# A two-stream decoder kernel: another merged order of the two streams' steps on every engine

## The reference

```python
# layer 0
x = LN(x + relu(softmax(causal(x Wq (x Wk)^T / 16))) (x Wv))             # "self"
x = LN(x + LN(softmax(mask(x Wq2 (ctx Wk2)^T / 16)) (ctx Wv2)) g + b)    # "cross"
x = LN(x + sign_mlp(x))            # 256 -> 1024 -> 1024 -> 256, weights +1/-1   "sign"
# layer 1
x = LN(x + causal_performer(x))    # 16 heads, 64 relu features, running sums   "perf"
x = LN(x + mlstm(x, ctx))          # 8 heads, exponential gates, group norm    "mlstm"
x = LN(x + ffn(x))                 # int8 rounding, 256 -> 1024, conv of 3, silu, -> 256  "quant"
```

## Time and profile before

| | |
|---|---|
| median of 3 runs | 868.52 us (868.14 to 871.88) |
| the profiled execution's own time | 874.67 us |
| its span, from the first to the last instruction | 873.4 us |
| PE busy | 757.4 us, 87% |
| DVE busy | 588.3 us, 67% |
| ACT / POOL busy | 368.2 us, 42% / 147.9 us, 17% |
| mean granted TensorE clock | 0.90 |

### The profile page before, as it was taken

How to read it: one execution, slowest core, us unless ns; L and a number is a source line. 1 busy time by engine, 2 the same in 40 slices (tenths; PEclk the granted TensorE clock), 3 DMA queues, 4 the chain that set the end, 5 groups by cost and what they waited for, 6 DMA issues and landing times.

```text
span 873.4 us, 14709 instructions
## 1 busy us (share of the span) xinstructions
PE 757.4 (87%) x5872; PEld 531.1 (61%) x5872; DVE 588.3 (67%) x1486; ACT 368.2 (42%) x659; POOL 147.9 (17%) x223
## 2 busy tenths in 40 slices
PE   9999999999999985779889999999999968668214
PEld 5776654575787774676564676676476846547102
DVE  2485864264546779987789856566365767778796
ACT  2564632123314625843338433343354125473183
POOL 5021100031000324102310020110014120113200
PEclk9999999999999995858899999999999968869565
DMA  9501000001000102003000030000000000000001
GB/s 353 189 1 73 1 1 0 1 2 44 8 2 2 26 1 73 25 25 96 1 1 0 2 96 2 2 1 2 1 2 1 2 1 2 0 2 2 0 12 36
DMA packets 12739, 23.75 MB, mean 27 GB/s; under 512 B 768, under 2 KB 7040, under 8 KB 12416
## 3 DMA queue, kind: packets, MB, share of 16 engines
q1 hardware_dynamic: 12672, 22.82, 7.6%
HBM read 20.72 MB, written 2.10 MB: 26 GB/s over the span
## 4 chain that ended last, share of the span: by engine, by line
PE 71%; DVE 20%; POOL 3%; issue 3%; ACT 2%; DVEq 0%; ACTq 0%
PE bank L719 13%; PE bank L543 7%; PE bank L535 5%; PE bank L567 5%; PE bank L588 5%; PE bank L810 3%; PE bank L729 3%; PE bank L792 3%; PE bank L707 2%; PE bank L760 2%; POOL small L2071 2%; DVE work L1630 2%; PE bank L1011 2%; DVE work L1624 2%; DVE stats L1121 1%
## 5 line engine op out<-in xcount | busy, mean ns | idle before, releaser
L2001 POOL TENSOR_TENSOR rstd<-rstd,minus_half 128x2 f32<-128x2 f32 x56 | 44.5, 795 | 458.7 <-DVE rstd L1127 458.5
L719 PE MATMUL bank<-work,f0w 128*128 128x512 f16 x512 | 112.8, 379 | 0.0
L719 PEld LDWEIGHTS bank<-work,f0w 128*128 128x128 f16 x512 | 50.1, 98 | 59.4 <-issue 0.8
L1337 DVE SCALAR_TENSOR_TENSOR work<-bank,work 128x512 f16<-128x512 f32 x64 | 42.2, 686 | 45.0 <-ACT work L1829 44.8
L1829 ACT ACTIVATE work<-bank 128x512 f16<-128x512 f32 x64 | 36.6, 596 | 74.8 <-PE bank L719 60.5
L588 PE MATMUL bank<-work 128*128 128x256 f32 x208 | 49.8, 382 | 0.0
L2071 POOL TENSOR_TENSOR small<-small,minus_half 128x8 f32<-128x8 f32 x16 | 27.7, 1729 | 105.2 <-DVE small L1560 105.2
L1011 PE MATMUL bank<-work 128*128 128x66 f32 (+1 forms) x256 | 36.8, 307 | 8.7 <-DVE work L1501 6.2
L1011 PEld LDWEIGHTS bank<-work 128*128 128x128 f32 x256 | 36.6, 227 | 10.3 <-issue 7.3
L588 PEld LDWEIGHTS bank<-work 128*128 128x128 f32 x208 | 37.4, 190 | 5.1 <-issue 0.8
L810 PE MATMUL bank<-work 64*128 64x128 f32 x512 | 38.7, 292 | 1.1 <-DVE work L1420 1.1
(11 more groups left out here) (296 smaller groups left out, 1771.4 us busy)
## 6 DMA issues: line engine op xcount, KB each, us to landing
work<-in_mask SPq DMA_DIRECT2D x4, 1024.0 KB, 8.8
xT<-in_xT SPq DMA_DIRECT2D x4, 512.0 KB, 5.2
ctxT<-in_ctxT SPq DMA_DIRECT2D x4, 512.0 KB, 5.9
perf_w<-in_k SPq DMA_DIRECT2D x3, 512.0 KB, 11.3
perf_w<-in_perf_w SPq DMA_DIRECT2D x1, 1536.0 KB, 6.0
ctx<-in_w SPq DMA_DIRECT2D x2, 512.0 KB, 14.0
work<-in_w SPq DMA_DIRECT2D x1, 1024.0 KB, 16.0
x<-in_x SPq DMA_DIRECT2D x2, 512.0 KB, 15.2
```

Of the source, the lines that this page charges most:

```text
L719: ins = nc.tensor.matmul(u.bank[:, :], f0w1[:, k, m * P:(m + 1) * P], s.h1[part][:, k, :], start=(k == 0 and part == 0), stop=(k == NF - 1 ...
L1337: low_part(what, m, dst, number + m, lambda o, x, hi: nc.vector.scalar_tensor_tensor(out=o, in0=x, scalar=0.0, in1=hi, op0=ALU.max, op1=AL ...
L2001: nc.gpsimd.tensor_tensor(s.rstd[:, two], s.rstd[:, two], minus_half[:, 0:2], ALU.pow).then_inc(s.rstd_made.sem, 1)
```

## The change

New texts for all five engines; nothing else. The diff's core, one line of each for two engines (the other lines are replaced in the same way):

```diff
 TURNS = {
     "tensor":
-        "a1 b1 a2 b3 a2 b1 a2 b1 a3 b1 a1 b2 a3 b4 a1 b1 a3 b3 a2 b2 a2 b3 a1 b5 a1 b5 a4 b1 a2 b2 a2 b3 a1 b7 a1 b1 "
+        "a5 b1 a6 b1 a2 b1 a5 b2 a2 b1 a13 b2 a1 b3 p1 a2 b2 a2 b2 a1 b1 a6 b1 a3 b2 a2 b1 a2 b1 a3 b1 a2 b3 a2 b1 a2 "
...
     "sync":
-        "w1 a1 w1 b1 w2 a1 w2 b1 w1 b2 a2 w1 a1 b1 a1 b1 a2 b2 a3 b3 a2 b2",
+        "w4 a1 w1 b1 a1 w1 a1 w1 b2 a1 b1 w1 b1 a6 b1 a1 b5 a2 b2",
```

More of the change, by code:

```diff
@@ L37 @@
     "tensor":
[8 rows of a table removed]
-    "vector":
[11 rows of a table removed]
-    "scalar":
[7 rows of a table removed]
[8 rows of a table added]
+    "vector":
[11 rows of a table added]
+    "scalar":
[8 rows of a table added]
     "gpsimd":
-        "a1 b1 a1 b1 a1 b5 a7 b1 a1 b3 a1 b1 a1 b1 a6 b3 a6 b3 a1 b1 a1 b3 a2 b1 a1 b1 a6 b1 a1 b1 a2 b3 a1 b4 a3 b2 "
-        "a1 b1 a1 b2 a5 b1 a2 b9 a1 b3 a1 b2",
+        "a7 b3 a5 b4 a4 b2 a1 b2 a1 b1 a5 b1 a2 b3 a2 b2 a2 b3 a1 b1 a1 b1 a3 b2 a1 b1 a1 b1 a3 b3 a1 b4 a3 b2 a1 b2 "
+        "a1 b1 a5 b1 a2 b10 a1 b2 a1 b2",
     "sync":
-        "w1 a1 w1 b1 w2 a1 w2 b1 w1 b2 a2 w1 a1 b1 a1 b1 a2 b2 a3 b3 a2 b2",
+        "w4 a1 w1 b1 a1 w1 a1 w1 b2 a1 b1 w1 b1 a6 b1 a1 b5 a2 b2",
 }
```

## The result

The changed kernel takes 866.4 us in the median of 20 runs (862.08 to 868.68), the old one 870.24 us (20 runs, 865.8 to 874.56). I had forecast 8 us, and 860.5.

A forecast was written before the change was run, and what follows sets the result against it. No single bound: sign and perf at PE's pace, mlstm and quant at DVE's. Gains of 5 us up to b1's start, 0 in the middle and 3 at the end made 8, from 868.5 to 860.5 us; range 846 to 876.

The forecast's parts named there:

- The step that failed: From b1's start at 516 to about 717 us: orders nearly the same, PE has work; 0, give or take 2 us.
- Term 1: The start: a0, nearly alone, reaches perf at about 133 us instead of 179.5, with 5 us added (bounds 2 and 12).
- The rival in which it loses 12 us: a0's lone start loses 12 us, not 5, using up the middle stretch's gain; within the no-difference rival, chance 0.22.
- Term 2: a0 through perf and mlstm: reaches `quant.turn0` at about 314 us instead of 345.3, 31 us earlier.
- Term 3: From a0's `quant.turn0` to b1's `self.score0`: most of the lead is lost, b1 starts 5 us earlier.
- Term 4: The end: a1's DVE work fills b1's gaps, 3 us earlier (bounds 0 and 7).
- the larger gain: The valley closes, DVE fed at 91% from a0's `quant.turn0` to b1's start; 845.5 us, chance 0.13.
- the slower one: a1's attention and b0's head steps hold each other up, DVE under 79% before b1's start; 878 us, chance 0.19.
- No difference that tells: Mixture before b1's start runs at 81%, or a0's lone start loses 12 us; about 867.5 us, chance 0.22.

The follow-up runs named there:

- e14: Changed kernel with the old order put back from a1's `quant.hidden0` to the end; ratio 1.0025 to the old kernel, 2.2 us slower.
- e1: Old kernel with the changed order only in round 0, up to b1's `self.q`; ratio 0.9972, 2.4 us faster.
- e4: Old kernel with the changed order in round 0 and from a1's `quant.hidden0` to the end, old between; ratio 0.9938, 5.4 us faster.
- e8: The old kernel run once more without edit, for a second trace; 870.24 us, span 869.0.
- e15: Changed kernel with the old order where b1's cross lies beside a1's perf, up to b1's `sign.a0`; ratio 0.9913 to the old kernel, 7.6 us faster.
- e13: Old kernel with the changed round 0, plus b1's `self.q` and `self.v` moved ahead on PE; ratio 0.9923, 6.7 us faster.
- S: Part of the change where b1's self lies beside a1's perf, up to b1's `cross.q1`; alone on the old kernel ratio 1.0046, 4.0 us slower.
- the two PE moves: On PE b1's `self.q` ahead of a1's `perf.xT0`, `self.v` ahead of `perf.v0` and `xT1`; alone on the old kernel ratio 1.0032, 2.8 us slower.
- H: Part of the change in round 0, up to b1's `self.q`; alone on the old kernel ratio 0.9972, 2.4 us faster.
- M: Part of the change from b1's `self.q` to a1's `quant.hidden0`; alone on the old kernel ratio 1.0089, 7.7 us slower.
- e3: Old kernel with the changed order only from a1's `quant.hidden0` to the end; ratio 0.9942, 5.0 us faster.
- T: Part of the change from a1's `quant.hidden0` to the end; alone on the old kernel ratio 0.9942, 5.0 us faster.

## Why the prediction missed

**The step that failed** is "From 516 to about 717 us both orders are the same but for steps moved by one or two places in a stretch in which PE has work: 0, give or take 2." Behind the new round 0 this part costs 4.6 us (e14 less e1), with the new tail as well 2.0 (changed kernel less e4), on the old order 7.7. The traces show it in the changed kernel: 4.9 us ahead at b1's `self.score0`, 0.2 at its `sign.a0`. The stretch between these two steps, all engines, first in e8, then in the changed kernel, then in e15:

```profile
512.90:594.00 81.10, 80.90 (x789) 56.91 (x788) 46.17 (x131) 29.50 (x62) 9.00 (x15) 1.00 0.01 1
...
508.00:594.00 86.00, 80.77 (x814) 57.79 (x820) 46.40 (x134) 29.49 (x61) 11.41 (x18) 1.00 0.01 2
...
508.50:592.00 83.50, 80.29 (x813) 57.69 (x821) 46.61 (x134) 29.52 (x61) 11.60 (x18) 1.00 0.01 2
```

PE is busy 80 to 81 us at full clock in all three, and idles 0.2, 5.2 and 3.2 us (some tenths of the last two can be matmuls whose record is missing). So in the old order PE did have work without a break, and "PE has work" was still no reason for zero: it had work because the steps were laid so that one stream's product covers the other's wait. e15 names one place and gives 4.2 us back. What e15 still idles, e13 does not (its lead is 5.5 us at `self.score0` and 5.8 at `sign.a0`), and up to there the two differ only in the other moves of S, on PE, DVE and ACT.

**Term 1** was right in kind. a0's `perf.xT0` came at 127.1 us, ahead of the forecast's 133 and of its lower bound: from 9.5 us to there PE is busy 116.1 of 117.6 us, so the lone start made PE idle 1.5 us, where I had added 5. The rival in which it loses 12 us is out.

**Term 2**: `quant.turn0` at 311.6 on PE and 312.65 on DVE, forecast 314. Right; some of term 1's surplus was used up.

**Term 3**: the place was right, the gain was not. DVE's share was 84%, as forecast, and b1's `self.score0` came at 508.0, 3 us ahead of the 511 forecast. But the 516.05 that I measured the gain from came from the trace with the spell at a lower clock at 410 to 440 us; in e8 it is 512.9. And 2.4 of the changed kernel's 4.9 us at this step are owed to the two PE moves, which are part of S (e1 has 2.5, e13 with the moves 5.5). H alone gives 2.4 us, half of the 5; only where M is new is it worth 5.5 or 6.4. How much of H is owed to PE's and DVE's order and how much to the new order of the loads on SP, no run parts.

**Term 4** was 3 us in the forecast; it measures 5.0 alone and 5.6 in the changed kernel, but 3.0 behind the new H with the old M, all within its bounds of 0 to 7. I had seen the idle times of 9.0 and 6.4 us and argued that the waits for `mlstm.pow` would use most of the gain up. In e3 the idle time of the gate chain's stretch falls from 9.15 to 2.96 us, and from 6.45 to 4.87 in the next. Of a1's `quant.down0` on PE I said that it costs nothing ahead of b1's `mlstm.out3`. In the new tail DVE's `qlast`, for which `down0` waits, stands behind `ratio3`, which needs `out3`: with the old order of the two on PE, the waits would form a ring and none would end, so no run has the new tail without this move, and its share in T is open.

**The sum**: in gains, and each part priced behind the ones ahead of it in the program, H 2.4, M -4.6, T 5.6 are 3.4 us, against 5, 0 and 3. (Such a chain of differences gives 3.4 in any order: H 2.4, T 3.0, M -2.0 does too.) The signs of two terms held. In every order of adding M is on the losing side. How much of the shortfall is then term 3's depends on the order: 2.6 us where H is taken first, 4.6 where T alone is taken ahead of it, none where M is. A further 1.7 us of the distance between 860.5 and 866.4 is the base: the three runs' median of 868.5 stood below the 870.24 of twenty.

**The rivals**: the larger gain (DVE at 91%) did not come, and the slower one (a1's attention steps against b0's heads, under 79%) neither; the stretch was fed at 84%. "No difference that tells" has the number nearest to the result, but by another way than its own. None of them named the place: b1's cross beside a1's perf.

## What to carry to other kernels

A step moved by one place in an in-order queue is free only if it did not cover a wait; for every moved step, look which `idle before` would open on its own engine between the two steps that it used to part. The price of such a move belongs to the gap that stands there and not to the move alone: the same two moves cost 2.8 us in one surrounding and gained 4.3 in another, so price a rewritten order in pieces cut where both orders have done the same work, in the surroundings that they will have. And before a term is sized by one trace, look whether that execution is a typical one.

## What was not expected of the hardware

Executions of one kernel fall into levels some 4 us apart (866.2, 870.3 and 874.7 us, beside e1 to e4) at granted clocks of 0.909, 0.902 and 0.901, and the traces compared differ by spells at the lower clock, of which one, at 410 to 440 us (0.89 against 1.00), moved all that follows by some 3 us. What decides between the levels no run tells. From 319 to 400 us the granted clock rose from 0.64 to 0.92 and PE was busy 9.3 us more, and yet H alone gained no more than 2.4 us. That fits DVE being the last to be waited for there, as the earlier trace rows had it, but no run shows it by itself.
